# A perceiver block: order of small loads and scaled constants at two stage starts

## The chip, the cores and the metric

The kernel runs on one core of a Trainium2 chip. Its time is device time in microseconds (us) for one execution, as a median of several runs. A profiler trace of one such execution gives the start and duration of every instruction; all clock times below count from the start of that trace's span.

## The reference

One latent array x (512 rows of 512) attends to a context of 8192 rows, and then passes a state-space block, an MLP and a routed mixture of experts. Only the first part bears on this change:

```python
q = (scale * (layernorm(x) @ Wq + bq)).reshape(bs, q_len, NH, DM)     # 512 queries, 16 heads of 64
k = (ctx @ Wk + bk).reshape(bs, kv_len, NH, DM)                        # 8192 keys
v = (ctx @ Wv + bv).reshape(bs, kv_len, NH, DM)
a = softmax(einsum('nlhd,nshd->nhls', q, k), axis=-1)
x = x + einsum('nhls,nshd->nlhd', a, v).reshape(bs, q_len, NH * DM) @ Wo + bo
x = x + mamba_block(layernorm(x))                                      # scales by norm1_w first
x = x + mixture_of_experts(x)
```

Every float32 operand of a product is split into a float16 high part and a float16 rest, so a product is three float16 matmuls.

## The kernel before

The program is a row of stages. Each stage is one block in which all five engines run their own instruction lists, tied together by semaphores. A `Space` owns a stage's semaphores. When the stage ends, GpSimd clears them and all engines meet at a barrier (`Space.clear`, line 57), so nothing of the next stage starts before the last engine of this one is through, SyncE's waits for its transfers included. The order of work on each engine is the order in which its function is written. All DMAs that matter here are issued by SyncE and share one queue, which serves them in the order of issue.

**Latent queries** (`latent_queries`, names `lq_*` in the trace). SyncE loads x whole (line 130), then six halves of Wq, Wk and Wv into three buffers `wf` (line 135), with the query bias `bqc` behind the second half. From the fourth half on, a load waits until VectorE has split what lay in its buffer. Behind the sixth half come the key bias `bkc` (line 138) and the first two context chunks `cf[0]` and `cf[1]` (line 140). VectorE takes the row statistics of x (`row_factor`), normalises, and makes the float16 rests. ScalarE makes the float16 high parts. TensorE transposes x and computes eight pairs of heads (96 matmuls). For each pair j, ScalarE writes `qf` and its high part `qh[j]`, and VectorE the rest `ql[j]` (line 208). After the pairs, ScalarE and VectorE split the first context chunk (`keep.ch[0]`, line 180; `keep.cl[0]`, line 215), and VectorE scales the key bias (`keep.bks`, line 213). SyncE stores `qh` and `ql` to `q_dram` in two rounds, then waits at the end for both context chunks (`c_in`) and for the four stores (`q_out`, line 147).

**Context keys and values** (`context_keys_values`, names `kv_*`). TensorE works without a pause through 16 chunks. Its first product waits for `ch_ready`, `cl_ready` and `kf_ready`. At the stage's start VectorE raises semaphores by hand, one after another, to say that buffers are free; `ch_ready` and `cl_ready` are the thirteenth and the fourteenth (lines 437 and 438), `kf_ready` the first.

**Attention** (`attention`, names `at_*`). Each of 16 heads runs 32 steps (HP). In a step TensorE computes scores of 256 keys into one of three PSUM slots `st`, ScalarE exponentiates them into one of four buffers `pf` (line 734), ScalarE or VectorE makes the high part `ph` (line 728 or 772), VectorE the rest `pl` (line 776), and TensorE multiplies them with the values, four steps at a time. TensorE runs: scores of four steps, then values of the four steps before (`step`, called by `turns`). VectorE and ScalarE run `pair_turns`: the first CUT = 20 steps of head 0 straight, and everything else in a hardware loop over pairs of heads. SyncE loads head 0's queries, then four quarters of head 0's keys and values, then the queries of the other 15 heads, then the value bias `bvc` and the norm weight `nw` (both on semaphore `vec_in`), the output bias `bob`, and last a fill of `xs_dram` with zeros. Only then comes its loop that loads the next head's keys and values. VectorE waits for `vec_in`, scales the two vectors (`bvs`, `nws`, lines 763 and 764) and only then starts with step 0; ScalarE waits for `consts` before its step 0 (line 744). The scaled vectors are read for the first time at the end of the second head (`high` and `low`) and at the stage's end.

## Time and profile before

| | us |
|---|---|
| median of three runs | 2627.29 |
| lowest, highest | 2626.81, 2628.77 |
| the profiled execution's own time | 2626.91 |
| its span, first to last instruction | 2625.2 |
| TensorE busy | 2409.1 (92%) |
| VectorE busy | 1976.4 (75%) |
| ScalarE busy | 1595.8 (61%) |
| GpSimd busy | 683.3 (26%) |

The busy times are sums over stages with different limits. TensorE is nearly always at work inside the context stage and inside attention. What the change touches lies at their starts, where its busy share falls: the page's row of TensorE in 40 slices of 65.6 us reads 6 in the first slice and 1 in the fourteenth. Clock times in the text refer to this trace.

### The profile page before, as it was taken

The page shows a single profiled execution, that of the slowest core. Times are in us where ns is not written, and L with a number is a line of the kernel's source. Part 1 is how long each engine was busy: PE and PEld are TensorE (multiplying, and loading weights), DVE is VectorE, ACT ScalarE, POOL GpSimd, SP SyncE. Part 2 cuts the span into 40 slices and gives each one's busy share as a digit, 9 for nine tenths or more (in the row PEclk, how much of TensorE's full clock was granted, in tenths as well). Part 3 has the DMA queues.
Part 4 walks back from the last instruction along what each step waited for, and adds up shares of the span by engine and source line. Part 5 has one row for each costly group of instructions (what it writes and reads, how often), then busy time and mean ns, then how long its engine had stood idle before and what let it go on. Part 6 is the DMA issues. An engine that isn't in the chain of part 4 may idle for free. (4 is left out here: it accounts for less than half of the span.)

```text
span 2625.2 us, 39371 instructions
## 1 busy us (share of the span) xinstructions
PE 2409.1 (92%) x14143; PEld 1016.7 (39%) x14143; DVE 1976.4 (75%) x1974; ACT 1595.8 (61%) x1962; POOL 683.3 (26%) x475
## 2 busy tenths in 40 slices
...
GB/s 240 81 158 169 185 144 156 207 148 144 194 126 81 190 171 97 108 100 99 94 104 96 88 115 93 104 96 57 109 162 1 0 0 192 49 195 324 391 379 129
DMA packets 175780, 366.01 MB, mean 139 GB/s; under 512 B 17313, under 2 KB 88097, under 8 KB 172001
## 3 DMA queue, kind: packets, MB, share of 16 engines
...
HBM read 254.24 MB, written 106.68 MB: 137 GB/s over the span
## 5 line engine op out<-in xcount | busy, mean ns | idle before, releaser
L447 DVE TENSOR_REDUCE kv_mx<-kv_s 128x1024 f32 (+1 forms) x512 | 595.5, 1217 | 227.0 <-PE kv_s L477 227.0
L776 DVE TENSOR_TENSOR at_pl<-at_pf,at_ph 128x1024 f16<-128x1024 f32 x512 | 613.1, 1223 | 109.2 <-ACT at_ph L728 100.4
L734 ACT ACTIVATE at_pf<-at_st 128x1024 f32<-128x1024 f32 x512 | 497.0, 1025 | 213.2 <-PE at_st L893 119.3
L892 PE MATMUL at_st<-keep_big,at_k_cur 128*128 (+1 forms) x1024 | 392.2, 383 | 48.8 <-ACT at_pf L734 30.9
L893 PE MATMUL at_st<-keep_big,at_k_one 128*128 (+1 forms) x1024 | 390.7, 382 | 0.0
L728 ACT ACTIVATE at_ph<-at_pf 128x1024 f16<-128x1024 f32 x256 | 273.0, 1066 | 0.0
L1068 POOL MEMSET mi_xp<- 128x24 f32 x1 | 0.1, 123 | 977.8 <-POOLq L60 977.8
L857 PE MATMUL at_acc<-at_ph,at_vs 128*128 128x512 f16 x1024 | 242.4, 379 | 1.5 <-DVE at_pl L776 1.4
L367 POOL TENSOR_TENSOR kv_ksl<-kv_kf,kv_ksh 128x512 f16<-128x512 f32 x128 | 147.9, 1156 | 247.2 <-ACT kv_ksh L395 247.2
L993 PE MATMUL kv_kp<-first_ch,first_wkh 128*128 128x512 f16 x512 | 194.9, 381 | 8.8 <-DVEq L438 8.8
L993 PE MATMUL kv_kp<-first_ch,first_wkl 128*128 128x512 f16 x512 | 194.9, 381 | 0.0
L993 PE MATMUL kv_kp<-first_cl,first_wkh 128*128 128x512 f16 x512 | 194.6, 380 | 0.0
L993 PE MATMUL kv_vp<-first_wvl,first_ch 128*128 128x512 f16 x512 | 194.6, 380 | 0.0
L993 PE MATMUL kv_vp<-first_wvh,first_ch 128*128 128x512 f16 x512 | 194.5, 380 | 0.0
L993 PE MATMUL kv_vp<-first_wvh,first_cl 128*128 128x512 f16 x512 | 194.2, 379 | 0.0
L392 ACT ACTIVATE kv_kf<-kv_kp,first_bks 128x512 f32<-128x512 f32 x128 | 87.3, 682 | 172.3 <-PE kv_kp L993 172.3
L399 ACT ACTIVATE kv_vf<-kv_vp 128x512 f32<-128x512 f32 x128 | 76.0, 594 | 184.3 <-PE kv_vp L993 184.3
L1362 PE MATMUL ms_yp<-ms_hc,ms_ident 128*128 128x512 f32 x256 | 137.4, 684 | 51.2 <-POOL ms_hc L1248 42.6
L892 PEld LDWEIGHTS at_st<-keep_big,at_k_cur 128*128 128x128 f16 x1024 | 100.5, 98 | 211.2 <-issue 56.0
L371 POOL TENSOR_TENSOR kv_vs<-kv_vf,kv_vs 128x512 f16<-128x512 f32 x128 | 147.9, 1155 | 129.5 <-ACT kv_vs L401 129.5
L772 DVE CAST at_ph<-at_pf 128x1024 f16<-128x1024 f32 x256 | 175.5, 685 | 0.0
L1264 POOL TENSOR_TENSOR ms_b<-ms_u,keep_big 128x1024 f32<-128x1024 f32 x64 | 149.0, 2349 | 0.6
...
## 6 DMA issues: line engine op xcount, KB each, us to landing
...
at_k_cur<-kd SPq DMA_DIRECT2D x128, 256.0 KB, 3.9
at_vs<-vd SPq DMA_DIRECT2D x64, 512.0 KB, 3.9
kv_tf<-wpack SPq DMA_DIRECT2D x21, 1024.0 KB, 6.3
keep_big<-down SPq DMA_DIRECT2D x17, 1024.0 KB, 10.4
first_cf<-ctxT SPq DMA_DIRECT2D x16, 1024.0 KB, 13.2
kd<-kv_ksh SPq DMA_DIRECT2D x32, 512.0 KB, 9.8
```

The lines of the kernel that those rows point to most:

```text
L367: nc.gpsimd.tensor_tensor(ksl[par][:, n, :], kf[:, n % 4, :], ksh[par][:, n, :], ALU.subtract).then_inc(kl_ready, 1)
L371: nc.gpsimd.tensor_tensor(vs[par][:, hs, kt, DH:2 * DH], vf[:, n % 4, :].rearrange("p (h d) -> p h d", d=DH), vs[par][:, hs, kt, 0:DH], AL ...
L447: nc.vector.reduce_max(mx[:, bass.ds(g * (NH * TT) + 2 * (m - TT), 2)], s1[:, m % 3, :, :], AX.X).then_inc(s1_max, 1)
L728: nc.scalar.activation(ph[:, s % RING, :, :], pf[:, s % FULL, :, :], ACT.Copy).then_inc(ph_ready, 1)
L734: nc.scalar.activation(pf[:, s % FULL, :, :], st[:, s % HP % NST, :, :], ACT.Exp, scale=SCORE).then_inc(pf_ready, 1)
L772: nc.vector.tensor_copy(ph[:, s % RING, :, :], pf[:, s % FULL, :, :]).then_inc(ph_own, 1)
L776: nc.vector.tensor_tensor(pl[:, s % RING, :, :], pf[:, s % FULL, :, :], ph[:, s % RING, :, :], ALU.subtract).then_inc(pl_ready, 1)
L857: nc.tensor.matmul(acc[:, 0, :], vs[:, 2 * s + e, :], ph[:, s % RING, e, :], start=(s == 0 and e == 0), stop=False)
L892: nc.tensor.matmul(st[:, w % NST, e, :], k_cur[:, tile], qh[:, q], start=True, stop=False)
L893: last = nc.tensor.matmul(st[:, w % NST, e, :], k_one[:, tile], ql[:, q], start=False, stop=True)
L993: last = nc.tensor.matmul(out, a, b, start=(start and n == 0), stop=(stop and n == len(pairs) - 1))
L1264: nc.gpsimd.tensor_tensor(b[i % RB][:, :, :], u[:, :].unsqueeze(1).to_broadcast([P, HN, T]), bb[q], ALU.mult).then_inc(b_ready, 1)
```

## The change

In the latent stage, x is loaded in four pieces with a semaphore each, and the statistics of a piece wait for that piece alone. The first context chunk is loaded behind `bqc`, ahead of the third weight half, and is split between the weight halves 1 and 2. The key bias keeps its place behind the sixth half, but VectorE now waits for it and scales it ahead of the eight pairs. The second context chunk's load has its own semaphore. `ql` is no tensor of its own any more; it lies in the second chunk's buffers `keep.ch[1]` and `keep.cl[1]`. The wait for the stores of the queries leaves the stage: `q_out` becomes a semaphore of the whole program, and ScalarE waits for it in the context stage before it overwrites `keep.ch[1]`. Its `Space`, `whole`, is closed at the very end of the program. At the start of the context stage, `ch_ready` and `cl_ready` are raised first. In attention, `bvc` and `nw` are loaded ahead of the other heads' queries, and both the scaling on VectorE and ScalarE's wait for it come behind the first 20 steps.

```diff
@@ -107,18 +107,18 @@
-        qh, ql = keep.qh, m.sb("ql", [P, PAIRS, T], F16)
+        qh, ql = keep.qh, [(keep.ch if j < 4 else keep.cl)[1][:, j % 4, :] for j in range(PAIRS)]
...
-        x_in, b_in, made = m.sem("x_in"), m.sem("b_in"), m.sem("made")
+        x_in, b_in, made = [m.sem(f"x_in{t}") for t in range(TT)], m.sem("b_in"), m.sem("made")
@@ -127,24 +127,28 @@
-            sp.dma_start(xs[:, :, :], x.rearrange("(t p) d -> p t d", p=P)).then_inc(x_in, 16)
+            def load_context(n, sem):
+                sp.dma_start(keep.cf[n][:, :, :], ctxT.rearrange("(c p) s -> p c s", p=P)[:, :, n * CK:(n + 1) * CK]
+                             ).then_inc(sem, 16)
+
+            for t in range(TT):
+                sp.dma_start(xs[:, t, :], x[t * P:(t + 1) * P, :]).then_inc(x_in[t], 16)
             for n, (w, cols) in enumerate(halves):
+                if n == 2:
+                    load_context(0, c_in)
                 if n >= 3:
                     sp.wait_ge(wl_ready, n - 2)
                 src = (wq, wk, wv)[w].rearrange("(c p) n -> p c n", p=P)
                 sp.dma_start(wf[n % 3][:, :, :], src[:, :, cols]).then_inc(w_in[n % 3], 16)
                 if n == 1:
                     sp.dma_start(bqc[:, :], bq).then_inc(b_in, 16)
-            sp.dma_start(keep.bkc[:, :], bk).then_inc(c_in, 16)
-            for n in range(2):
-                sp.dma_start(keep.cf[n][:, :, :], ctxT.rearrange("(c p) s -> p c s", p=P)[:, :, n * CK:(n + 1) * CK]
-                             ).then_inc(c_in, 16)
-            for js in (slice(0, 4), slice(4, 8)):
+            sp.dma_start(keep.bkc[:, :], bk).then_inc(bk_in, 16)
+            load_context(1, next_in)
+            for js, low in ((slice(0, 4), keep.ch[1]), (slice(4, 8), keep.cl[1])):
                 sp.wait_ge(ql_ready, js.stop)
-                for s, q in enumerate((qh, ql)):
-                    sp.dma_start(q_dram[s].rearrange("(j p) t -> p j t", p=P)[:, js, :], q[:, js, :]).then_inc(q_out, 16)
-            sp.wait_ge(c_in, 48)
-            sp.wait_ge(q_out, 64)
+                for s, q in enumerate((qh[:, js, :], low[:, :, :])):
+                    sp.dma_start(q_dram[s].rearrange("(j p) t -> p j t", p=P)[:, js, :], q).then_inc(keep.q_out, 16)
+            sp.wait_ge(next_in, 16)
 
@@ -164,6 +168,8 @@
             split(1)
+            act.wait_ge(c_in, 16)
+            nc.scalar.activation(keep.ch[0][:, :, :], keep.cf[0][:, :, :], ACT.Copy, scale=SA).then_inc(ch_ready, 1)
             split(2)
@@ -176,8 +182,6 @@
                     split(3 + j // 2)
-            act.wait_ge(c_in, 48)
-            nc.scalar.activation(keep.ch[0][:, :, :], keep.cf[0][:, :, :], ACT.Copy, scale=SA).then_inc(ch_ready, 1)
@@ -189,8 +193,7 @@
-            dve.wait_ge(x_in, 16)
-            row_factor(nc, dve, own, xs, *rows.all, var_ready, sd_ready, 1, 1e-5, False)
+            row_factor(nc, dve, own, xs, *rows.all, var_ready, sd_ready, 1, 1e-5, False, x_in)
@@ -202,19 +205,18 @@
             split(1)
+            dve.wait_ge(ch_ready, 1)
+            nc.vector.scalar_tensor_tensor(keep.cl[0][:, :, :], keep.cf[0][:, :, :], SA, keep.ch[0][:, :, :],
+                                           ALU.mult, ALU.subtract)
             split(2)
+            dve.wait_ge(bk_in, 16)
+            nc.vector.tensor_scalar(keep.bks[:, :], keep.bkc[:, :], SA, None, ALU.mult)
             for j in range(PAIRS):
...
-                nc.vector.tensor_tensor(ql[:, j, :], qf[:, j % 4, :], qh[:, j, :],
+                nc.vector.tensor_tensor(ql[j], qf[:, j % 4, :], qh[:, j, :],
...
                     split(3 + j // 2)
-            dve.wait_ge(c_in, 48)
-            nc.vector.tensor_scalar(keep.bks[:, :], keep.bkc[:, :], SA, None, ALU.mult)
-            dve.wait_ge(ch_ready, 1)
-            nc.vector.scalar_tensor_tensor(keep.cl[0][:, :, :], keep.cf[0][:, :, :], SA, keep.ch[0][:, :, :],
-                                           ALU.mult, ALU.subtract)
@@ -403,6 +405,8 @@
                         nxt = 1 - par
+                        if i is None:
+                            act.wait_ge(keep.q_out, 64)
                         act.wait_ge(c_in[nxt], 16 * (uses + 1) + 16 * par)
@@ -424,6 +428,8 @@
+            dve.sem_inc(ch_ready, 1)
+            dve.sem_inc(cl_ready, 1)
             dve.sem_inc(kf_ready, 2)
@@ -434,8 +440,6 @@
                 dve.sem_inc(c_in[par], 16)
-            dve.sem_inc(ch_ready, 1)
-            dve.sem_inc(cl_ready, 1)
             for e in range(TW):
@@ -615,9 +619,9 @@
                 load_values(0, q)
-            load_queries(1, NH, q_rest_in)
             sp.dma_start(bvc[:, :], bv).then_inc(vec_in, 16)
             sp.dma_start(nw[:, :], n1w).then_inc(vec_in, 16)
+            load_queries(1, NH, q_rest_in)
             sp.dma_start(bob, bo.partition_broadcast(P)).then_inc(small_in, 16)
@@ -697,12 +701,13 @@
-        def pair_turns(eng, step, end, late):
+        def pair_turns(eng, step, end, late, once):
...
             for s in range(CUT):
                 step(0, s)
+            once()
             with eng.Fori(0, PAIRS - 1) as j:
@@ -741,8 +746,7 @@
-            act.wait_ge(consts, 2)
-            pair_turns(act, pair, lambda h: None, {HIGH_AT: high})
+            pair_turns(act, pair, lambda h: None, {HIGH_AT: high}, lambda: act.wait_ge(consts, 2))
@@ -759,10 +763,11 @@
             dve.sem_inc(o_out, 48)
-            dve.wait_ge(vec_in, 32)
-            nc.vector.tensor_scalar(bvs[:, :], bvc[:, :], SA, None, ALU.mult).then_inc(consts, 1)
-            nc.vector.tensor_scalar(nws[:, :], nw[:, :], SA, None, ALU.mult).then_inc(consts, 1)
-            dve.wait_ge(consts, 2)
+            def scaled():
+                dve.wait_ge(vec_in, 32)
+                nc.vector.tensor_scalar(bvs[:, :], bvc[:, :], SA, None, ALU.mult).then_inc(consts, 1)
+                nc.vector.tensor_scalar(nws[:, :], nw[:, :], SA, None, ALU.mult).then_inc(consts, 1)
+                dve.wait_ge(consts, 2)
@@ -803,7 +808,7 @@
-            pair_turns(dve, pair, end, {SUMS_AT: reciprocals, SCALE_AT: scale, LOW_AT: low})
+            pair_turns(dve, pair, end, {SUMS_AT: reciprocals, SCALE_AT: scale, LOW_AT: low}, scaled)
@@ -945,10 +950,12 @@
-def row_factor(nc, dve, own, src, st, mv, var, sd, rs, tmp, var_ready, sd_ready, n, eps, rms):
+def row_factor(nc, dve, own, src, st, mv, var, sd, rs, tmp, var_ready, sd_ready, n, eps, rms, rows_in=None):
 
 
     for t in range(TT):
+        if rows_in:
+            dve.wait_ge(rows_in[t], 16)
         own.inc(nc.vector.bn_stats(st[:, t, :], src[:, t, :]))
@@ -2150,6 +2157,8 @@
+    ending = ExitStack()
+    whole = Space(nc, ending, "whole")
@@ -2158,6 +2167,7 @@
+        keep.q_out = whole.sem("q_out")
@@ -2179,6 +2189,7 @@
         experts(nc, keep, xs_dram, ys_dram, wsplit, gate_up, down, out)
+    ending.close()
```

The rows below are the engines' instruction lists, before and after. Names in brackets are semaphores by the physical one that they share, so a name there can come from an earlier stage.

SyncE in the latent stage, from the query bias on, before:

```order
L137 DMA lq_bqc<-bq 128x8
L135 DMA lq_wf<-wk 128x4x512
L135 DMA lq_wf<-wk 128x4x512 [waits lq_wl_ready]
L135 DMA lq_wf<-wv 128x4x512 [waits lq_wl_ready] x2
L138 DMA first_bkc<-bk 128x8
L140 DMA first_cf<-ctxT 128x4x512 x2
L145 DMA q_dram<-first_qh 128x4x512 [waits lq_ql_ready]
L145 DMA q_dram<-lq_ql 128x4x512
L145 DMA q_dram<-first_qh 128x4x512 [waits lq_ql_ready]
L145 DMA q_dram<-lq_ql 128x4x512
L99 UNCONDITIONAL_BRANCH [waits lq_q_out,lq_c_in]
```

And after:

```order
L144 DMA lq_bqc<-bq 128x8
L131 DMA first_cf<-ctxT 128x4x512
L142 DMA lq_wf<-wk 128x4x512
L142 DMA lq_wf<-wk 128x4x512 [waits lq_wl_ready]
L142 DMA lq_wf<-wv 128x4x512 [waits lq_wl_ready] x2
L145 DMA first_bkc<-bk 128x8
L131 DMA first_cf<-ctxT 128x4x512
L150 DMA q_dram<-first_qh 128x4x512 [waits lq_ql_ready]
L150 DMA q_dram<-first_ch 128x4x512
L150 DMA q_dram<-first_qh 128x4x512 [waits lq_ql_ready]
L150 DMA q_dram<-first_cl 128x4x512
L99 UNCONDITIONAL_BRANCH [waits lq_next_in]
```

One context chunk now stands ahead of three weight halves, and at the stage's end the wait for the stores (`lq_q_out`) is gone.

VectorE in the latent stage, from the second weight half to the end of the stage, before:

```order
L189 SCALAR_TENSOR_TENSOR lq_wl<-lq_wf1,lq_wh 128x4x512 [waits lq_wh_ready]
L189 SCALAR_TENSOR_TENSOR first_wkl<-lq_wf2,first_wkh 128x4x512 [waits lq_wh_ready]
L208 TENSOR_TENSOR lq_ql<-lq_qf,first_qh 128x512 [waits lq_qh_ready] x2
L189 SCALAR_TENSOR_TENSOR first_wkl<-lq_wf0,first_wkh 128x4x512 [waits lq_wh_ready]
L208 TENSOR_TENSOR lq_ql<-lq_qf,first_qh 128x512 [waits lq_qh_ready] x2
L189 SCALAR_TENSOR_TENSOR first_wvl<-lq_wf1,first_wvh 128x4x512 [waits lq_wh_ready]
L208 TENSOR_TENSOR lq_ql<-lq_qf,first_qh 128x512 [waits lq_qh_ready] x2
L189 SCALAR_TENSOR_TENSOR first_wvl<-lq_wf2,first_wvh 128x4x512 [waits lq_wh_ready]
L208 TENSOR_TENSOR lq_ql<-lq_qf,first_qh 128x512 [waits lq_qh_ready] x2
L213 TENSOR_SCALAR first_bks<-first_bkc 128x8 [waits lq_c_in]
L215 SCALAR_TENSOR_TENSOR first_cl0<-first_cf0,first_ch0 128x2048 [waits lq_ch_ready]
```

And after (`first_ch1` and `first_cl1` are where `ql` lies now):

```order
L193 SCALAR_TENSOR_TENSOR lq_wl<-lq_wf1,lq_wh 128x4x512 [waits lq_wh_ready]
L209 SCALAR_TENSOR_TENSOR first_cl0<-first_cf0,first_ch0 128x2048 [waits lq_ch_ready]
L193 SCALAR_TENSOR_TENSOR first_wkl<-lq_wf2,first_wkh 128x4x512 [waits lq_wh_ready]
L213 TENSOR_SCALAR first_bks<-first_bkc 128x8 [waits lq_bk_in]
L216 TENSOR_TENSOR first_ch1<-lq_qf,first_qh 128x512 [waits lq_qh_ready] x2
L193 SCALAR_TENSOR_TENSOR first_wkl<-lq_wf0,first_wkh 128x4x512 [waits lq_wh_ready]
L216 TENSOR_TENSOR first_ch1<-lq_qf,first_qh 128x512 [waits lq_qh_ready] x2
L193 SCALAR_TENSOR_TENSOR first_wvl<-lq_wf1,first_wvh 128x4x512 [waits lq_wh_ready]
L216 TENSOR_TENSOR first_cl1<-lq_qf,first_qh 128x512 [waits lq_qh_ready] x2
L193 SCALAR_TENSOR_TENSOR first_wvl<-lq_wf2,first_wvh 128x4x512 [waits lq_wh_ready]
L216 TENSOR_TENSOR first_cl1<-lq_qf,first_qh 128x512 [waits lq_qh_ready] x2
```

The split of the chunk moves in among the weight halves, and the scaling of the key bias stands with its wait ahead of the first pair.

VectorE at the start of attention, from its barrier on, before (`kv_v_out1` is `vec_in`, `kv_v_out0` is `consts`):

```order
L753 UNCONDITIONAL_BRANCH [waits barrier_Pool_Activation_PE_DVE_SP_release]
L756 MEMSET keep_big 64x4096
L763 TENSOR_SCALAR at_bvs<-at_bvc 128x8 [waits kv_v_out1]
L764 TENSOR_SCALAR at_nws<-at_nw 128x4
L776 TENSOR_TENSOR at_pl<-at_pf,at_ph 128x1024 [waits lq_q_ready,kv_v_out0]
L772 CAST at_ph<-at_pf 128x1024 [waits lq_ql_ready,lq_b_ready]
L776 TENSOR_TENSOR at_pl<-at_pf,at_ph 128x1024 [waits lq_qf_ready]
```

And after, the same place:

```order
L757 UNCONDITIONAL_BRANCH [waits barrier_Pool_Activation_PE_DVE_SP_release]
L760 MEMSET keep_big 64x4096
L781 TENSOR_TENSOR at_pl<-at_pf,at_ph 128x1024 [waits lq_wl_ready]
L777 CAST at_ph<-at_pf 128x1024 [waits lq_q_ready,lq_wh_ready]
L781 TENSOR_TENSOR at_pl<-at_pf,at_ph 128x1024 [waits lq_own_dve]
```

VectorE after, around its twentieth step (the branch is the entry of the loop over pairs of heads):

```order
L777 CAST at_ph<-at_pf 128x1024 [waits lq_q_ready,lq_wh_ready]
L781 TENSOR_TENSOR at_pl<-at_pf,at_ph 128x1024 [waits lq_own_dve]
L768 TENSOR_SCALAR at_bvs<-at_bvc 128x8 [waits kv_v_out1]
L769 TENSOR_SCALAR at_nws<-at_nw 128x4
L711 UNCONDITIONAL_BRANCH [waits kv_v_out0]
L711 ISA
L781 TENSOR_TENSOR at_pl<-at_pf,at_ph 128x1024 [waits lq_wl_ready]
```

The two scalings move from the front to behind the twentieth step, and the wait for them now stands at the entry of the loop (the same on ScalarE).

## Rows read from the trace of the kernel before

**Rows 1.** Waits, 850 to 930 us: engine, waiting for what, total us, times, longest.

```profile
DVE at_bvs L763 <- DMA at_nw<-n1w: 38.3, 1, 38.3
ACT at_pf L734 <- DVE at_nws L764: 31.9, 1, 31.9
```

**Rows 2.** Timeline, attention start: start us, duration, engine, line, operation [idle before].

```profile
889.17 1.28 ACT L734 ACT_TABLE_LOAD   x1 [19.46 <-PE at_st L893]
891.90 14.83 SPq L597 DMA_DIRECT2D keep_big<-q_dram  x3
...
922.10 0.17 DVE L763 TENSOR_SCALAR at_bvs<-at_bvc 128x8 f32<-128x8 f32 x1 [38.34 <-DMA at_nw<-n1w]
922.38 1.94 ACT L734 ACTIVATE at_pf<-at_st 128x1024 f32<-128x1024 f32 x2 [31.92 <-DVE at_nws L764]
```

**Rows 3.** DMA issues at 911.43 and 913.38 us: KB each, us to landing.

```profile
at_nw<-n1w SPq DMA_DIRECT2D x1, 2.0 KB, 10.6
...
xs_dram<-at_none SPq DMA_DIRECT2D x1, 5888.0 KB, 23.7
```

**Rows 4.** DMA issue at 884.15 us, the first quarter of head 0's values.

```profile
at_vs<-vd SPq DMA_DIRECT2D x1, 512.0 KB, 6.2
```

**Rows 5.** Timeline: head 0's first product with values; exponentials of steps 32, 33.

```profile
929.87 0.38 PE L857 MATMUL at_acc<-at_ph,at_vs 128*128 128x512 f16 x1
...
977.80 1.94 ACT L734 ACTIVATE at_pf<-at_st 128x1024 f32<-128x1024 f32 x2 [1.48 <-DVE at_pl L776]
```

**Rows 6.** Timeline in a steady stretch of attention: VectorE, ScalarE, TensorE.

```profile
1021.21 1.22 DVE L776 TENSOR_TENSOR at_pl<-at_pf,at_ph 128x1024 f16<-128x1024 f32 x1
...
1020.56 1.94 ACT L734 ACTIVATE at_pf<-at_st 128x1024 f32<-128x1024 f32 x2 [1.48 <-DVE at_pl L776]
...
1022.01 0.38 PE L892 MATMUL at_st<-keep_big,at_k_cur 128*128 x1
```

**Rows 7.** GpSimd by lines, 879 to 896 us (busy us, mean ns); VectorE's timeline.

```profile
L680 POOL MEMSET at_k_one<- 64x2048 f16 x4 | 7.2, 1799 | 0.2
...
880.28 3.47 DVE L756 MEMSET keep_big<- 64x4096 uint32 x1 [11.42 <-PEq L60]
```

**Rows 8.** Timeline of VectorE in the first half of the latent stage.

```profile
6.45 2.47 DVE L952 BATCH_NORM_STATS2 lq_st<-lq_xs 128x6 f32<-128x512 f32 x4 [6.45 <-DMA lq_xs<-x]
...
12.72 0.16 DVE L198 TENSOR_SCALAR lq_bqs<-lq_bqc 128x8 f32<-128x8 f32 x1
...
18.85 2.29 DVE L189 SCALAR_TENSOR_TENSOR lq_wl<-lq_wf,lq_wh 128x2048 f16<-128x2048 f32 x1 [1.11 <-ACT lq_wh L158]
21.06 2.28 DVE L189 SCALAR_TENSOR_TENSOR first_wkl<-lq_wf,first_wkh 128x2048 f16<-128x2048 f32 x1
```

**Rows 9.** DMA issues at 2.41 us and at 23.4 us (the last weight half).

```profile
lq_bqc<-bq SPq DMA_DIRECT2D x1, 4.0 KB, 9.6
...
lq_wf<-wv SPq DMA_DIRECT2D x1, 1024.0 KB, 5.5
```

**Rows 10.** Timeline, latent stage's last pair to the next stage's first product.

```profile
38.31 0.38 PE L993 MATMUL lq_qp<-lq_xh,lq_wl 128*128 128x512 f16 x1
...
40.11 0.69 DVE L208 TENSOR_TENSOR lq_ql<-lq_qf,first_qh 128x512 f16<-128x512 f32 x1 [0.49 <-ACT first_qh L176]
...
41.23 0.51 SPq L145 DMA_DIRECT2D q_dram<-lq_ql  x1
...
46.14 0.20 POOL L75 MEMSET kv_ident<- 128x128 f32 x1 [44.60 <-POOLq L60]
...
47.49 0.58 PE L993 MATMUL kv_kp<-first_ch,first_wkh 128*128 128x512 f16 x1 [8.80 <-DVEq L438]
```

**Rows 11.** Waits of SyncE's queue between 0 and 60 us.

```profile
SPq L147 <- DMA q_dram<-lq_ql: 3.4, 1, 3.4
```

**Rows 12.** Windows: length, busy us of PE, PEld, DVE, ACT, POOL, granted clock, DMA.

```profile
38.70:43.00 4.30, 0.00 (x0) 0.00 (x0) 2.79 (x5) 3.11 (x3) 0.00 (x0) 1.00 0.30 99
...
47.40:50.00 2.60, 2.51 (x6) 0.87 (x7) 0.00 (x0) 0.00 (x0) 0.00 (x0) 0.50 0.76 306
```

4 lines of the change are left out of this document (2 added, 2 removed).

## The prediction

> **What bounds the kernel now.** Inside the context stage and inside attention TensorE runs without gaps, so only starts and ends of stages can give time back. I read the list of waits at the two places that the change touches, then the timeline there, then the transfers' times to landing.
>
> At the start of attention the list shows two waits in a chain [rows 1]: VectorE stands 38.3 us until `nw` lands, and ScalarE 31.9 us for VectorE's two small scalings. The reader is to see in the timeline [rows 2] that everything else was ready: ScalarE loads its exponential table at 889.17, right after the first scores, is done with it at 889.17 + 1.28 = 890.45, and starts the first exponential at 922.38. The cause is the queue. The queries of the 15 other heads are issued from 891.90 on and take 14.83 us to issue alone [rows 2], and `nw` lands 911.43 + 10.6 = 922.0 [rows 3]. TensorE can fill three slots and then waits as well.
>
> At the seam between the first two stages [rows 10] TensorE ends its last pair at 38.31 + 0.38 = 38.7 and starts the context stage at 47.49. What ends this: the last store of `ql` is issued by 41.74, SyncE waits 3.4 us for its landing [rows 11], 45.1; the barrier takes until 46.14; then VectorE raises fourteen semaphores by hand before TensorE may go, until 47.49.
>
> **Attention: the scalings leave the front.** The first exponential then waits only for its scores and the table: 890.45 in place of 922.38, **-31.9 us**. What is late next must not be a transfer. Head 0's own loads are issued before the moved ones and keep their times. The first product with values ran 929.87 - 922.38 = 7.5 us behind the first exponential [rows 5], so it comes at 897.9, and its quarter of values lands at 884.15 + 6.2 = 890.4 [rows 4]: 7.5 us of slack. Head 1's first keys are needed just before step 32, which ran at 977.80, 55.4 us behind the first exponential [rows 5], so at some 946. SyncE cannot issue them before it is through with the queries and the zero fill. The fill lands at 913.38 + 23.7 = 937.1 [rows 3] and is bound by bytes, not by issue, so it stays there; three quarter loads of 256 KB behind it need some 3 us, by half the 6.2 us of the 512 KB load [rows 4]. That is 940, 6 us in time. Moved with the fronts are only two tiny loads. Bounds: -30 (TensorE is still at half clock for a part of this) to -32.5.
>
> **Attention: the wait stands behind step 19 now.** On VectorE two operations of 0.17 us and their waits, 922.38 - 922.10 = 0.28 us [rows 2], come behind its twentieth step; queued behind them are its steps 20 on. ScalarE waits there for VectorE, which it otherwise never does this closely: in the steady rhythm ScalarE starts a new group of four at 1020.56 while VectorE ends the last step of the group before only at 1021.21 + 1.22 = 1022.43 [rows 6]. Step 20 opens a group. So its exponential starts at 1022.43 + 0.28 on that scale, 2.15 us late. TensorE's fourth score pair of that group needs it: it ran at 1022.01, and the exponential (half of 1.94, some 1.0) would have been done at 1021.6, 0.4 us earlier. So 1.75 us reach TensorE, which has no gap to win them back. The entry of the hardware loop, so far covered by ScalarE's idle 1.48 us per group, stands behind this wait too; I add 0.45 for it, between 0 and 1.5. Together **+2.2**, bounds 0.4 (if the rhythm at step 20 is looser than at step 60) and 3.3.
>
> **Latent stage: what ends it.** The pieces of x let VectorE take the statistics while x lands. The last piece lands when all of x does, at 6.45; three of four statistics of 2.47 us are then done, and the normalised rows come 1.85 us earlier. But the scaling of `bqc` at 12.72 waits for its load, 2.41 + 9.6 = 12.0 [rows 8, 9], so VectorE's chain behind it gains 0.7, at most 0.9 in TensorE's start. The stage's end does not see it, because of the new wait for `bk_in` on VectorE. `bkc` is issued behind the last weight half, in the same queue. That half was issued at 23.4, just behind VectorE's split of the third half (21.06 + 2.28), and took 5.5 us [rows 8, 9]. After the change VectorE has one chunk more to split there (2.21 us from start to start, 18.85 to 21.06) and starts some 1.9 earlier, so the half is issued at about 23.8 and lands at 29.3, `bkc` a little before or behind it; I take 29.0. Until then VectorE stands, with all eight `ql` and three weight splits queued behind: 8 x 0.60 + 3 x 2.21 = 11.4 us (from start to start: 0.69 less the 0.08 by which neighbours overlap at 21.06), so the last `ql` ends at 29.0 + 0.1 + 11.4 + 0.1 = 40.6. Before, it ended at 40.11 + 0.69 = 40.8 [rows 10]. TensorE and ScalarE pass this place with room (pair 7's `qf` needs only the `ql` of pair 3). So the end of the last `ql` moves by **-0.2**, bounds -0.9 (`bkc` lands early) and +1.0 (2 us late, half of it hidden). ScalarE's added 1.9 us of chunk split is hidden by its idle time between pairs.
>
> **The seam.** The stores are issued by 41.6 as before, but nothing waits for them: VectorE's 2.29 us and ScalarE's 1.89 us on the first chunk were under that wait already and are gone from the end as well. The barrier took 1.0 us from the last landing [rows 10, 11], so the context stage starts at 42.6 in place of 46.14: -3.4, besides the -0.2 above which is in it. The order of the hand-raised semaphores: fourteen took 47.49 - 46.14 = 1.35 us, of which three are left, 0.3: -1.05. Sum of latent stage and seam **-4.5**, bounds -3.3 and -5.7. The wait for `q_out` in the context stage comes on ScalarE behind its first key and value tile, some 8 us into the stage, when the stores (3.4 us) have landed: nothing.
>
> **Clock at the seam.** TensorE's pause shrinks from 8.8 to about 5 us. The granted clock was 1.00 in the first 4.3 us of the pause and 0.50, the lower of its levels of 1.2 and 2.4 GHz, when work resumed: six matmuls in 2.6 us instead of 1.3 [rows 12]. I count no change; if the shorter pause keeps the clock, 1.3 us more are won.
>
> **The end.** `whole` is cleared at the very end: one more clearing and one more barrier behind the last store. By the seam above at most 1.0 us; I take **+0.8**, bounds 0.3 and 1.0.
>
> **A rule weighed against the rows.** VectorE's casts and rests of the first steps, from about 892 on, now meet GpSimd's memsets, which run to 896. Rows 7 show VectorE's memset of 3.47 us from 880.28 across two or three of GpSimd's, while the four of line 680 take 1.80 us each on the mean, touched or not: no sign that one holds up the other, so the sum has 0 for it. The Trainium skill, SBUF — State Buffer, section "SBUF: two separate sides", says of the port pair that VectorE and GpSimd share that it is an exclusive lock and that whoever comes second blocks until the first is done. By that rule the first cast could wait for one memset.
>
> **Sum.** -31.9 + 2.2 - 4.5 + 0.8 = -33.4. From the profiled execution's own 2626.9 that is 2593.5; the median of the runs is 0.4 above it, so **2593.9 us**, 1.3% faster.
>
> **Rivals.**
> - Transfers become the bound of head 0 or of head 1's start. For it: the queue is full from 881 to 937, and the shortest slack is 6 us. Against it: what is needed first is issued first and keeps its place. If the fill and the keys behind it came 14 us late, 8 would show: 2602.
> - A lock between VectorE and GpSimd at 892 to 896, the rule above: one memset of 1.80 us [rows 7] on VectorE, 2595.7.
> - The clock stays up over the shorter seam: 2592.6.
> - The first exponential waits for something that the list of waits hides, since a wait for several semaphores is put down to the last of them, and the change at attention doesn't do what it says. Then only the rest is left: 2626.9 - 4.5 + 2.2 + 0.8 + 0.4 = 2625.8, no change. Against it: the table load, behind the scores' semaphore, started at 889.17.
> - Slower: the pushed wait at step 20 throws three engines out of their rhythm and they settle in a slower one. Steady groups have TensorE without a gap, and ScalarE 1.48 us idle. From a loss of 0.27 us per group over the 123 groups behind step 20 the gain is gone; at 0.35 the time is 2593.9 + 43 = 2637. Against it: three slots and four buffers take up such a push, and TensorE's order is fixed.
>
> **Chances.** Forecast 0.75, clock stays 0.08, lock 0.05, transfers 0.07, does not act 0.02, slower rhythm 0.03. A measurement here can tell about 0.2%, 5 us, from no change. Faster 0.95, same 0.02, slower 0.03. Range: the sum of the good bounds, -32.5 + 0.4 - 5.7 + 0.3 = -37.5, with 1.3 of clock less, would be 2588.5, of the bad ones -30 + 3.3 - 3.3 + 1.0 = -29.0, 2598.3. Not all fall on one side, and a part of the transfers' case is let in above: 2589.5 to 2600.
>
> **What would show it.** The wait list at the start of attention has no row of 31.9 us; ScalarE's first exponential starts 1.3 us behind the first scores. Before step 20's exponential ScalarE idles some 3.5 to 4 us for VectorE. VectorE idles about 5 us in the latent stage ahead of `bks`, and the first product of the context stage starts near 43. Wrong would be: keys or values named before TensorE in heads 0 and 1, or idle time of TensorE in every group of four.

## The result, and the profile after

The changed kernel takes **2593.12 us** in the median of four runs (2591.79 to 2599.14), the kernel before 2628.03 on the same chip (2626.81 to 2629.07). The ratio is 0.9872, with a 95% interval of 0.9855 to 0.9889: 1.3% faster. On a second chip it was 2596.09 against 2628.09, ratio 0.9879 (0.9863 to 0.9896). The profiled execution took 2591.8 us, its span 2590.1.

The list of waits at the start of attention in the changed kernel, first 876 to 930 us (engine, line, waiting for what: total us, times, longest):

```profile
PE at_st L897 <- DMA keep_big<-m_dram: 18.8, 1, 18.8
POOL at_ones L681 <- POOLq L60: 17.7, 1, 17.7
DVE at_pl L781 <- ACT at_ph L733: 16.0, 5, 10.2
ACT at_pf L739 <- PE at_st L898: 14.5, 5, 9.5
...
ACT at_pf L739 <- DVE at_nws L769: 3.8, 1, 3.8
```

The two waits of [rows 1], 38.3 and 31.9 us, are gone. What ScalarE waits for now are the scores, and once, for 3.8 us, the scaled vectors. The timeline of SyncE, ScalarE and GpSimd there:

```profile
889.67 0.43 SPq L623 DMA_DIRECT2D at_nw<-n1w  x1
890.14 13.59 SPq L601 DMA_DIRECT2D keep_big<-q_dram  x3
...
908.91 0.71 SPq L627 DMA_DIRECT2D xs_dram<-at_none  x1
910.02 17.28 SPq L607 DMA_DIRECT2D at_k_cur<-kd  x2
```

```profile
887.55 1.02 ACT L739 ACTIVATE at_pf<-at_st 128x1024 f32<-128x1024 f32 x1 [9.48 <-PE at_st L898]
889.25 1.02 ACT L739 ACTIVATE at_pf<-at_st 128x1024 f32<-128x1024 f32 x1 [0.68 <-PE at_st L898]
```

The stage starts at 876.62 (GpSimd's first row, below), 2.74 us earlier than before, and the first exponential at 887.55 in place of 922.38. The keys of head 1 stand behind the zero fill in the queue, issued from 910.02 on. The list above ends before they are needed; the same list taken for 876 to 1100 us has no wait of TensorE for keys or values either, only 18.8 us for `m_dram` at the start, 2.1 for exponentials and 0.2 for rests. Around step 20, ScalarE and VectorE:

```profile
919.90 1.08 ACT L733 ACTIVATE at_ph<-at_pf 128x1024 f16<-128x1024 f32 x1
924.76 1.94 ACT L739 ACTIVATE at_pf<-at_st 128x1024 f32<-128x1024 f32 x2 [3.78 <-DVE at_nws L769]
```

```profile
923.10 1.23 DVE L781 TENSOR_TENSOR at_pl<-at_pf,at_ph 128x1024 f16<-128x1024 f32 x1
924.24 0.16 DVE L768 TENSOR_SCALAR at_bvs<-at_bvc 128x8 f32<-128x8 f32 x1
924.32 0.16 DVE L769 TENSOR_SCALAR at_nws<-at_nw 128x4 f32<-128x4 f32 x1
927.68 1.23 DVE L781 TENSOR_TENSOR at_pl<-at_pf,at_ph 128x1024 f16<-128x1024 f32 x1 [3.20 <-ACT at_ph L733]
```

The vectors landed long before; VectorE scales them as soon as it is through with step 19, and ScalarE, which had run ahead of it, has stood 3.78 us by then.

Latent stage and seam, VectorE and then TensorE and SyncE:

```profile
9.59 1.92 DVE L198 TENSOR_SCALAR lq_xn<-lq_xs,lq_mv,lq_rs 128x512 f32<-128x512 f32 x4
12.71 0.17 DVE L201 TENSOR_SCALAR lq_bqs<-lq_bqc 128x8 f32<-128x8 f32 x1 [1.20 <-DMA lq_bqc<-bq]
...
29.72 0.17 DVE L213 TENSOR_SCALAR first_bks<-first_bkc 128x8 f32<-128x8 f32 x1 [5.26 <-DMA first_bkc<-bk]
...
41.53 0.69 DVE L216 TENSOR_TENSOR first_cl<-lq_qf,first_qh 128x512 f16<-128x512 f32 x1 [0.48 <-ACT first_qh L182]
```

```profile
17.52 0.61 PE L1000 MATMUL lq_qp<-lq_xh,lq_wh 128*128 128x512 f16 x1 [2.22 <-DVE lq_xl L205]
17.92 0.63 PE L1000 MATMUL lq_qp<-lq_xl,lq_wh 128*128 128x512 f16 x1
...
44.57 0.38 PE L1000 MATMUL kv_kp<-first_ch,first_wkh 128*128 128x512 f16 x1 [4.46 <-DVEq L433]
```

```profile
42.65 0.51 SPq L150 DMA_DIRECT2D q_dram<-first_cl  x1
```

The first product of the context stage comes at 44.57, before at 47.49 [rows 10]. `bqs` is made at 12.71, where it was made before at 12.72 [rows 8]: in spite of the pieces of x nothing is won there. The first eight matmuls of the pairs stand 0.40 to 0.43 us apart, twice the 0.22 of before. A window at the start of the context stage (length, busy us, granted clock, DMA share, GB/s) has ten matmuls in 3.40 us at a granted clock of 0.50, the lower level:

```profile
44.90:48.30 3.40, 3.40 (x10) 1.22 (x8) 0.00 (x0) 0.00 (x0) 0.00 (x0) 0.50 1.02 318
```

### The profile page after: what moved, and what is told of

The parts are those of the page before. It is cut to its first block and busy times, and to the rows that moved or that the text cites. A ratio compares the mean times of both kernels' runs of the same rounds, so it can differ in the third digit from the quotient of the medians.

```text
span 2590.1 us, 39386 instructions
## 1 busy us (share of the span) xinstructions
PE 2405.5 (93%) x14143; PEld 1015.6 (39%) x14143; DVE 1976.4 (76%) x1974; ACT 1596.4 (62%) x1962; POOL 683.5 (26%) x475
## 5 line engine op out<-in xcount | busy, mean ns | idle before, releaser
L897 PE MATMUL at_st<-keep_big,at_k_cur 128*128 (+1 forms) x1024 | 391.3, 382 | 20.8 <-DMA keep_big<-m_dram 18.8
```

The lines of the kernel that those rows point to most:

```text
L897: nc.tensor.matmul(st[:, w % NST, e, :], k_cur[:, tile], qh[:, q], start=True, stop=False)
```

## The accounts

Each row below is a difference between two traces, read off the timelines; the first column is the trace shown ahead of the prediction against the one above, the second a pair taken together on the second chip (the runs `before_again` and `after_again` below). "Step n" is the start of ScalarE's exponential of step n.

| | predicted | first pair | second pair |
|---|---|---|---|
| latent stage and seam, to the first product | -4.5 | -2.92 | -5.07 |
| from there to attention's start | 0 | +0.18 | +0.54 |
| attention's start to step 0 | -31.9 | -32.09 | -33.67 |
| steps 0 to 16 | 0 | +0.93 | +0.81 |
| steps 16 to 24 | +2.2 | +1.88 | +1.88 |
| step 24 to the mixer's start | 0 | +0.61 | +0.42 |
| mixer, its output, experts, to the end | +0.8 | -3.69 | -1.41 |
| span | -33.4 | -35.1 | -36.5 |

The last row but one holds the extra barrier: from the issue of the last store to the end it was 2625.2 - 2622.0 = 3.2 before and is 2590.1 - 2586.5 = 3.6 now, **+0.4**. The rest of it, about -4.1 in the first pair, is in stages that the change doesn't touch. The row above it (+0.61, +0.42) lies within the scatter of that stretch, which took 909.8 to 910.8 us in all 14 traces. The second row has a cause, the clock: from the first product on, the context stage works at half clock for 2.7 us in the trace of before (47.49 to 50.15) and 3.4 in the changed kernel (to 48.31), and for 3.3 and 4.8 us in the second pair. Half of the differences, 0.4 and 0.7, is what that should cost, by estimate.

## Experiments

### The two parts, each alone

`e1_attention_only` has the changed attention (the loads of `bvc` and `nw` ahead, the scaling behind 20 steps) and the old latent stage, seam and end; `e2_latent_only` has the rest of the change and the old attention. The diff is that of `e2` against the changed kernel, without VectorE's part, whose scalings go back to the front as well:

```diff
-            sp.dma_start(bvc[:, :], bv).then_inc(vec_in, 16)
-            sp.dma_start(nw[:, :], n1w).then_inc(vec_in, 16)
             load_queries(1, NH, q_rest_in)
+            sp.dma_start(bvc[:, :], bv).then_inc(vec_in, 16)
+            sp.dma_start(nw[:, :], n1w).then_inc(vec_in, 16)
...
-            pair_turns(act, pair, lambda h: None, {HIGH_AT: high}, lambda: act.wait_ge(consts, 2))
+            act.wait_ge(consts, 2)
+            pair_turns(act, pair, lambda h: None, {HIGH_AT: high})
```

> Only the attention part of the change: the two small loads ahead of the other heads' queries, the scalings and ScalarE's wait behind step 19. The latent stage, the hand-raised semaphores and the end are those of before. Theory (the gain is the wait of the first exponential, less a push at step 20): the first exponential some 11 us behind the start of the attention stage in place of 43, one idle of ScalarE of 3.8 us ahead of step 20, and a gain at step 24 of 29 to 30 us; time 2596 to 2599 from 2628. Rival (the latent part carries more than its 3 us, say by what it does to later stages): 2601 or more here.

> Only the latent part of the change with the semaphores' order and the semaphore of the whole program; attention is that of before. Theory: the context stage's first product 2.9 us earlier, or up to 4.5 where TensorE's clock rises in the latent stage as early as before the change; 0.4 back at the end; time 2623.5 to 2625.5 from 2628, so hardly more than the runs scatter. Rival (the whole change scatters because this part disturbs the clock): runs spread over more than 3 us here.

Attention alone: ratio 0.9901 (0.988 to 0.9922). Latent stage, seam and end alone: 0.9979 (0.9968 to 0.9991). The product is 0.9880, the whole change 0.9872 and 0.9879: the parts add up within these intervals. Two numbers did not come as expected. The median of `e1` is 2601.49 us (four runs, 2597.15 to 2605.08), outside the 2596 to 2599 of its theory and inside its rival's 2601 or more. And the ten runs of `e2` spread over 8.9 us, which its rival had as the sign of a disturbed clock; the kernel before spreads over 10.1 us in 13 runs on the same chip, so the spread says nothing of the change. The times alone leave `e1` a gain between 20 and 32 us; that attention carries its 30 is shown by the traces. In them the first exponential of `e1` comes 9.54 us behind the stage's start (before: 43.02), and step 24 comes 53.85 us behind it, where before it took 84.19 and 84.86, so 30.3 to 31.0 us less; the first product of `e2` comes at 44.95, where the two kernels with the old stage, `e1` and `before_again`, have 49.73 and 49.81.

### Is it the order of the loads, or the place of the scaling?

`e3_old_loads` is the changed kernel with `bvc` and `nw` loaded behind the other heads' queries again (the first two lines of the diff above). `e4_front_scaling` keeps them ahead, and scales and waits ahead of step 0 again (the last lines of it).

> The changed kernel with the two small loads put back behind the 15 heads' queries; the scalings stay behind step 19. Theory (putting the scalings late is what acts): nw lands some 43 us behind the start of the attention stage, as before the change, and VectorE asks for it at 47.6, so ScalarE's idle time ahead of step 20 stays 3.8 us and the time is that of the changed kernel within its scatter, 2591 to 2599. Rival (the order of loads acts too): ScalarE idles longer than 5 us ahead of step 20, and the time rises by that.

> The changed kernel with the scalings and the wait for them back at the front of attention; the two small loads stay ahead of the other heads' queries. Theory (the queue serves in order of issue): nw is issued behind head 0's quarters and lands with the last of them, some 27 to 29 us behind the start of the stage, so the first exponential starts there in place of 11 (changed) and 43 (before). There is no push at step 20. Time 2591.8 + 17 - 2.8, some 2606 to 2608. Rival (small loads overtake large ones): the first exponential at 11 to 15, 2590.

`e3` starts step 0 10.88 us behind the stage's start, as the changed kernel does (10.93), and reaches step 24 at 931.00 against 931.53: the order of the loads gives nothing once the scaling is late. `e4` starts it 28.93 us behind. Its ScalarE and VectorE:

```profile
906.01 1.94 ACT L738 ACTIVATE at_pf<-at_st 128x1024 f32<-128x1024 f32 x2 [17.46 <-DVE at_nws L768]
```

```profile
905.73 0.17 DVE L767 TENSOR_SCALAR at_bvs<-at_bvc 128x8 f32<-128x8 f32 x1 [24.26 <-DMA at_nw<-n1w]
```

In `e4` `nw` is issued at 890.26 and its scaling starts at 905.73, 15.5 us later, for 2 KB: it lands behind head 0's keys and values, which are in the queue ahead of it. So of the 32 us, loading first would have won 14 and scaling late wins all. Each was run once, in 2599.65 us (`e3`, expected 2591 to 2599) and 2611.01 (`e4`, expected 2606 to 2608); both times came out above what was expected, and the reading rests on the traces.

### The push at step 20

`e5_wait_at_use`: ScalarE waits for the constants where it reads them.

```diff
             def high(j):
+                act.wait_ge(consts, 2)
...
-            pair_turns(act, pair, lambda h: None, {HIGH_AT: high}, lambda: act.wait_ge(consts, 2))
+            pair_turns(act, pair, lambda h: None, {HIGH_AT: high}, lambda: None)
```

> The changed kernel with one move: ScalarE no longer waits for the scaled constants behind step 19 but inside `high`, where it reads them first; VectorE scales them behind step 19 as before. Theory: the longer four steps before step 20 (9.44 us for steps 16 to 20 in the changed kernel, 7.20 before) are ScalarE's wait for VectorE, so here steps 16 to 20 take 7.2 us, steps 20 to 24 take 7.1, and step 24's exponential comes 1.9 us nearer to the stage's start. Rival: VectorE's queue is what is late, and the steps stay at 9.4 or the same 2 us show in the next four. In the total 1.9 us, 0.07%, which may not be told from the scatter of later stages.

```profile
923.97 1.06 ACT L733 ACTIVATE at_ph<-at_pf 128x1024 f16<-128x1024 f32 x1
924.92 1.94 ACT L739 ACTIVATE at_pf<-at_st 128x1024 f32<-128x1024 f32 x2
```

ScalarE goes from step 19 into step 20 without a pause. Steps 16 to 20 take 7.20 us and 20 to 24 7.13, as before the change (7.20 and 7.13; changed kernel 9.44 and 6.77). The push is ScalarE's wait and nothing else, 1.88 us; VectorE's two operations in the same place (923.86 and 923.94) cost nothing. In the total it can't be seen: ratio 0.9882 (0.9865 to 0.9898).

### The latent stage

`e7_x_whole` loads x in one DMA. `e8_bias_early` loads both biases right behind x:

```diff
+            sp.dma_start(bqc[:, :], bq).then_inc(b_in, 16)
+            sp.dma_start(keep.bkc[:, :], bk).then_inc(bk_in, 16)
             for n, (w, cols) in enumerate(halves):
...
-                if n == 1:
-                    sp.dma_start(bqc[:, :], bq).then_inc(b_in, 16)
-            sp.dma_start(keep.bkc[:, :], bk).then_inc(bk_in, 16)
```

> The changed kernel with x loaded by one DMA, as before. Theory: the pieces bring the normalised rows 1.3 us nearer, but VectorE waits 1.0 to 1.2 us for the query bias behind them, so loading whole costs 0 to 0.3 us: the split of the first weights starts at 12.7 to 13.1 and the first pair at 17.5 to 18.0. Rival: the pieces do bring the first pair forward by the 0.7 to 0.9 us of the prediction, and it starts at 18.3 or later here.

> The changed kernel with one move: both biases, `bqc` and `bkc`, are loaded right behind x, ahead of all weights. Theory: the pieces of x gave nothing because VectorE then waited 1.20 us for `bqc`, and the key bias cost VectorE 5.26 us ahead of the pairs because it stands behind six weight halves. Then neither wait shows here; the split of the first weights and TensorE's first pair start 0.7 to 1.1 us earlier than 17.5, at 16.4 to 16.8, or the weights become the bound, if two small loads ahead of them delay them by as much. The scaled key bias stands near 24 instead of 29.7, and the stage's end moves by the pairs' start alone, since the last rests of the queries wait for ScalarE. Rival: the 5.26 us of standing make the stage's end late; then the end moves by 2 us or more.

> The kernel before, traced once more. Asked: whether the trace shown above is typical at the eight pairs, whose matmuls stood 0.22 us apart from the first one on there and 0.43 us apart for the first eight in the changed kernel. Theory: the half clock from about 17.5 to 21 us depends on the execution and not on how x is loaded (the kernel with the attention part alone, which loads x whole, has it too), so it can show here; then the pairs last 22.5 to 23 us instead of 20.9 and the first product starts near 49 to 49.5. Rival: loading x whole keeps the clock up, and the pairs last 20.9 us again. Later stages give a spread: from the mixer's start to the output stage 296 to 299 us, experts to the end 302 to 310.

| trace | first pair starts | pairs end | took | last `ql` ends | behind the pairs |
|---|---|---|---|---|---|
| before | 17.80 | 38.69 | 20.9 | 40.80 | 2.11 |
| `before_again` | 17.94 | 41.01 | 23.1 | 43.12 | 2.11 |
| `e1` (old latent stage) | 18.00 | 40.93 | 22.9 | 43.04 | 2.11 |
| after | 17.52 | 40.12 | 22.6 | 42.22 | 2.10 |
| `after_again` | 17.70 | 40.29 | 22.6 | 42.39 | 2.10 |
| `e7_x_whole` | 17.96 | 38.86 | 20.9 | 42.56 | 3.70 |
| `e8_bias_early` | 16.79 | 39.37 | 22.6 | 41.47 | 2.10 |

Three things follow. **The clock.** The same code ran the pairs in 20.9 and in 23.1 us (before, `before_again`). The difference is the spacing of the matmuls at the start of the pairs, of the first ten here and of the first eight to thirteen in other traces:

```profile
17.94 0.61 PE L993 MATMUL lq_qp<-lq_xh,lq_wh 128*128 128x512 f16 x1 [1.42 <-DVE lq_xl L202]
18.34 0.63 PE L993 MATMUL lq_qp<-lq_xl,lq_wh 128*128 128x512 f16 x1
```

```profile
17.96 0.39 PE L999 MATMUL lq_qp<-lq_xh,lq_wh 128*128 128x512 f16 x1 [1.42 <-DVE lq_xl L204]
18.19 0.38 PE L999 MATMUL lq_qp<-lq_xl,lq_wh 128*128 128x512 f16 x1
```

The first two rows are `before_again`, the last two `e7`. Where the record of the granted clock reaches back so far, the wide spacing is the lower level: in `after_again` 0.50 from 18.8 to 22.1 us, 1.00 before and behind. Of 14 traces 12 have the wide spacing near the start of the pairs, in four of them only from the third to sixth matmul on, and their pairs last 22.5 to 23.7 us; the trace shown ahead of the prediction is one of the two that haven't. It made the latent stage of before look 2.2 us shorter than it is most of the time. Loading x whole isn't the reason, for `before_again` and `e1` load it whole too.

**The pieces of x** brought the first pair 0.24 to 0.28 us forward (17.96 and 17.94 against 17.70; 17.80 against 17.52), not 0.7 to 0.9: `bqc` landed when VectorE had already waited 1.20 us for it. Even the 0.28 can't be told from scatter, for the eight traces with x in pieces and the biases in their places start the first pair at 16.57 to 18.02, the four with x whole at 17.80 to 18.00. The pieces themselves push `bqc`: SyncE issues three more DMAs ahead of it, so that it is issued at 3.71 instead of 2.41. With the biases ahead (`e8`) that wait is gone and another takes its place, for the weights that now come behind two small loads. VectorE, ScalarE and SyncE of `e8`, and SyncE of the changed kernel:

```profile
10.67 0.17 DVE L200 TENSOR_SCALAR lq_bqs<-lq_bqc 128x8 f32<-128x8 f32 x1
12.04 2.29 DVE L192 SCALAR_TENSOR_TENSOR lq_wl<-lq_wf,lq_wh 128x2048 f16<-128x2048 f32 x1 [1.21 <-ACT lq_wh L161]
```

```profile
10.10 1.91 ACT L161 ACTIVATE lq_wh<-lq_wf 128x2048 f16<-128x2048 f32 x1 [2.38 <-DMA lq_wf<-wq]
```

```profile
3.63 0.98 SPq L144 DMA_DIRECT2D lq_wf<-wq  x2
```

```profile
2.68 0.98 SPq L142 DMA_DIRECT2D lq_wf<-wq  x2
```

From the start of ScalarE's first split, which follows the landing of the first weights, to the first pair it takes 6.69 us in `e8` (and in `e9` below), and 7.71 to 7.75 in the eight traces with the changed order: the wait for `bqc` was worth 1.0. But the first weights are issued 0.95 us later, at 3.63 instead of 2.68, so nearly all of it is given back on the way. `e8` starts its pairs at 16.79, as expected, yet that lies inside the 16.57 to 18.02 of the changed order; in one execution a gain of this size can't be seen.

**The wait for the key bias** was expected to show or not, by theory, in the stage's end. Both happened. In `e7`, at full clock, VectorE works without a pause from `bks` to the last `ql`:

```profile
30.98 0.17 DVE L212 TENSOR_SCALAR first_bks<-first_bkc 128x8 f32<-128x8 f32 x1 [5.27 <-DMA first_bkc<-bk]
31.06 1.29 DVE L215 TENSOR_TENSOR first_ch<-lq_qf,first_qh 128x512 f16<-128x512 f32 x2
...
41.27 1.29 DVE L215 TENSOR_TENSOR first_cl<-lq_qf,first_qh 128x512 f16<-128x512 f32 x2
```

That is 42.56 - 30.98 = 11.58 us, and the last `ql` ends 3.70 us behind the pairs instead of 2.11: the wait costs 1.6. A part of that is `e7`'s own, since `bks` comes 1.26 us later there than in the changed kernel (30.98 against 29.72). At full clock the changed kernel's pairs would end near 17.52 + 20.9 = 38.4, and the wait would cost some 0.8 (an estimate: 29.72 + 11.58 = 41.3 against 38.4 + 2.1). In the changed kernel and `after_again`, with the slow start of the pairs, the queue has caught up at the last pair and the wait costs nothing; `e8`, which has no such wait, ends its last `ql` just as far behind the pairs (2.10).

### The seam

`e10_q_wait` puts SyncE's wait for the four stores back; `e11_sems_late` puts the two hand-raised semaphores back behind twelve others.

```diff
             sp.wait_ge(next_in, 16)
+            sp.wait_ge(keep.q_out, 64)
...
-            dve.sem_inc(ch_ready, 1)
-            dve.sem_inc(cl_ready, 1)
             dve.sem_inc(kf_ready, 2)
...
                 dve.sem_inc(c_in[par], 16)
+            dve.sem_inc(ch_ready, 1)
+            dve.sem_inc(cl_ready, 1)
```

> The changed kernel with the wait for the four stores of the queries put back at the end of the latent stage. Theory: the stage's end stands behind the last store's landing; from the last rest of the queries to the next stage's start 5.3 us instead of 1.98, so 3.4 us later there (start near 47.6 for rests that end near 42.2) and 3.4 us in the total. Rival: the second context chunk, whose wait stays in both, lands last, and the start of the next stage moves by less than 1 us.

> The changed kernel with the two hand-raised semaphores for the first context chunk put back behind twelve others. Theory: the first product starts 0.37 us behind the stage's start in the changed kernel and 1.35 us before it, and this order alone is the difference; so 1.3 to 1.4 us here. Rival: the earlier product comes from the shorter wait list of TensorE or from the barrier, and it stays near 0.4.

`e10`, SyncE's last store, GpSimd's first row of the next stage, TensorE's first product; then GpSimd and TensorE in `e11`:

```profile
43.72 0.51 SPq L150 DMA_DIRECT2D q_dram<-first_cl  x1
...
48.81 0.20 POOL L75 MEMSET kv_ident<- 128x128 f32 x1 [47.27 <-POOLq L60]
...
49.19 0.59 PE L1001 MATMUL kv_kp<-first_ch,first_wkh 128*128 128x512 f16 x1 [8.01 <-DVEq L434]
```

```profile
45.46 0.20 POOL L75 MEMSET kv_ident<- 128x128 f32 x1 [43.91 <-POOLq L60]
...
46.81 0.59 PE L1000 MATMUL kv_kp<-first_ch,first_wkh 128*128 128x512 f16 x1 [5.43 <-DVEq L442]
```

From the last `ql` to the next stage it is 5.52 us with the wait (`e10`), 1.98 without (after), 5.34 before. From the stage's start to the first product it is 1.35 us with the old order (`e11`, and before) and 0.37 with the new one. Both edits do what they were costed at. One trace each; their totals (2603.57 and 2592.53 us, a single run) can't tell 1 us. In `e10` the first context chunk is loaded and split early and the seam is as long as before, so the early split wins nothing as long as the wait for the stores stands. The other half, no wait and the split still at the stage's end, was not run.

### A version of both

> The changed kernel once more, beside the next one on one chip. Theory: 1.3% faster than before, ratio 0.985 to 0.989. In the trace the marks of the first 930 us lie within 1 us of the first one's, the later stages scatter by some us.

> The changed kernel with ScalarE's wait for the constants at their first use and both biases loaded right behind x. Theory: 1.9 us from the push at step 20 and 0 to 0.3 us from the biases, ratio to before 0.0007 lower than that of the changed kernel, which is inside both intervals; in the trace steps 16 to 20 take 7.2 us and VectorE stands for neither bias. Rival: the two edits give more than their sum because VectorE's work in the latent stage gets 5.3 us of room, which brings the end of that stage forward; then the next stage starts at 43.0 or earlier relative to pairs that start at 17.5.

`e9_best` (the edits of `e5` and `e8` together) has a median of 2595.72 us and a ratio of 0.9874 (0.9858 to 0.9891), the changed kernel beside it 2596.09 and 0.9879 (0.9863 to 0.9896): not told apart. The 1.9 us at step 20 are won (steps 16 to 20 in 7.21), and in this execution the first weights landed later still, ScalarE's split of them starting at 11.98, so that the first pair started at 18.67, again 6.69 us behind. They took 8.3 us from issue to landing, against 6.4 in `e8` and 6.1 to 7.6 with the changed order; what delayed them stays open.

## Who holds up whom: VectorE and GpSimd

The prediction had 0 for a lock between VectorE and GpSimd, and a rival at 1.8 us. The traces show it. GpSimd and VectorE in the changed kernel:

```profile
876.62 0.12 POOL L681 MEMSET at_ones<- 128x32 f16 x1 [17.69 <-POOLq L60]
...
889.80 1.80 POOL L685 MEMSET at_k_one<- 1x2048 f16 x1
891.65 0.96 POOL L686 MEMSET at_none<- 128x1024 f16 x1
...
892.91 0.53 POOL L77 TENSOR_SCALAR_AFFINE_SELECT at_ident<-at_ident 128x128 f32<-128x128 f32 x1 [0.16 <-POOL at_ident L75]
```

```profile
891.25 1.23 DVE L781 TENSOR_TENSOR at_pl<-at_pf,at_ph 128x1024 f16<-128x1024 f32 x1 [10.25 <-ACT at_ph L733]
892.40 0.91 DVE L777 CAST at_ph<-at_pf 128x1024 f16<-128x1024 f32 x1
```

and in `after_again`:

```profile
892.36 1.42 POOL L686 MEMSET at_none<- 128x1024 f16 x1
...
894.09 1.35 POOL L77 TENSOR_SCALAR_AFFINE_SELECT at_ident<-at_ident 128x128 f32<-128x128 f32 x1 [0.16 <-POOL at_ident L75]
```

```profile
892.21 0.69 DVE L777 CAST at_ph<-at_pf 128x1024 f16<-128x1024 f32 x1
892.93 2.36 DVE L781 TENSOR_TENSOR at_pl<-at_pf,at_ph 128x1024 f16<-128x1024 f32 x2
```

In the first the memset was there first (891.65 to 892.61), and the cast ends 0.69 us behind it, its own length: 893.30. In the second the cast was there first (892.21 to 892.90), and the memset, 0.96 us long when alone, takes 1.42. The identity's select, which reads SBUF, takes 0.29 us when alone (before). In the first trace it came while the cast ran and takes 0.53, in the second it came while the second rest ran and takes 1.35; both times it ends 0.14 us behind the VectorE operation. But a rest of 1.23 us beside a memset of 1.80 stretches neither (891.25 and 889.80 above). The Trainium skill, SBUF — State Buffer, section "SBUF: two separate sides", says just that when read to its end: the lock is taken by a VectorE operation in a two-port mode against any GpSimd operation, and by one with two SBUF inputs only against a GpSimd operation that reads SBUF. The traces agree, with the numbers above; that the cast ran in such a mode no trace shows.

What it costs can be read from ten traces with the late scaling, since the memset of `at_none` starts 15.03 to 15.04 us behind the stage's start in all of them. Where the first cast was issued before it (`e1`, `e7`, `e10`, `e11`, `after_again`), step 16 starts 37.64 to 37.71 us behind the stage's start. Where it was issued with it or later (after, `e3`, `e5`, `e8`, `e9`), the cast ends at 16.68, however early it was issued, and step 16 starts at 38.70, **1.05 us later**. So 0.14 us between two casts (14.90 in `e10`, 15.04 in `e9`) decide on a microsecond. The first casts of `e9` and `e1`:

```profile
893.10 1.64 DVE L777 CAST at_ph<-at_pf 128x1024 f16<-128x1024 f32 x1
```

```profile
895.97 1.22 DVE L773 CAST at_ph<-at_pf 128x1024 f16<-128x1024 f32 x1
```

The stretch of the cast beyond its own 0.69 is the lock's own share: 0.95 us in `e9` (1.64), 0.92 in `e5` (1.61), 0.84 in `e8`, 0.55 in `e3`, and 0.22 in the changed kernel's first trace, whose cast came at 15.78 anyway. The memset ahead of `at_none` can hold it up too: in `e1` the cast was issued at 14.30 beside the last one of `at_k_one` (13.17 to 14.97) and took 1.22, 0.53 over its own, in `e7` 0.92 and in `e11` 0.78. In the traces where `at_none` came second, the late select holds up the second cast, 0.78 instead of 0.69. So the lock takes 0.1 to 1 us, never the 1.8 of the rival. No kernel with the memset elsewhere was run.

With this the 16 steps can be added up. In all 14 traces step 16 starts 22.02 to 22.12 us behind the end of the first cast, before and after. From step 0 to the start of that cast it takes 4.13 us where three slots of scores stand full (before, `before_again`, `e2`, `e4`) and 4.85 in the two traces of the changed kernel. That is +0.72 for the scores and +0.22 for the lock in the first, +0.72 and +0.1 in the second, which are the +0.93 and +0.81 of the table.

## Why the prediction was right, step by step

- **What bounds attention's start, right.** First exponential -31.9 predicted, -32.09 and -33.67 measured. It follows the first scores, which themselves start 9.00 us behind the stage's start instead of 7.85 in the first trace (8.09 against 8.17 in the second pair). The table load, taken as part of the path with its 1.28 us, is no longer on it: in the changed kernel it stands right at the stage's start, at 876.78. So -32.09 is luck in part, two misses of 1.28 and 1.15 us against each other; where the scores came as early as before, the gain was 33.67, outside the bounds of -30 to -32.5.
- **Not in the sum: the ramp.** Steps 0 to 16 take 0.8 to 0.9 us more. Before, three slots of scores stood full and the first exponentials ran back to back [rows 2]; now the second waits 0.68 for its scores, at half clock (granted clock 0.50 from 862 to 890), which gives 0.72, and VectorE meets GpSimd. The bound of -30 on the first term had left room for it, the value taken had not. The lock was priced at 0 and took 0.22 in the profiled execution, 0.1 to 0.95 in others. The step that failed is the reading of [rows 7] as no sign of it: they show a VectorE memset, not the cast that would stand there.
- **Push at step 20, right:** +2.2 predicted, +1.88 measured, 1.75 of it worked out from the steady rhythm. The 0.45 for the loop's entry is not needed; `e5` shows 7.20 and 7.13 with the entry in its place.
- **Latent stage, size off.** `ql` end -0.2 predicted, +1.42 measured against the trace shown, and -0.73 for `after_again` against `before_again`. With it the sum of latent stage and seam, -4.5 with bounds -3.3 and -5.7, came at -2.92, outside, and at -5.07. The working of VectorE's queue was right where it was tried: 11.5 to 11.6 us from `bks` to the end predicted, 11.58 in `e7`. `bkc` landed at 29.7, not 29.0. The step that failed is that this queue ends the stage. In the changed kernel it would have been through at 41.3, and TensorE's last pair, 22.6 us behind the first instead of 20.9, ended it at 42.2. What was missing is that the pairs' clock is not the same in each execution, and that it decides which of the two ends the stage.
- **x in pieces, wrong:** 0.7 to 0.9 predicted for the first pair, 0.24 to 0.28 measured; `bqc` was taken to land at 12.0 as before and landed at 12.7. That step overlooked what the pieces do to SyncE's own list, where they put `bqc` 1.3 us back.
- **Seam, right:** from the last `ql` to the next stage 2.0 us predicted (40.6 to 42.6), 1.98 measured, 5.34 before; semaphores -1.05 predicted, -0.98 measured. The prediction's own difference, 42.6 against 46.14, is -3.5, and its sum goes on with -3.4. **The clock there:** counted as no change. The first matmul ran at full clock, and then half clock lasted for more of the work than before, 3.4 us instead of 2.7. The rival, a clock that stays up, did not come.
- **End:** +0.8 predicted, +0.4 measured.
- **Transfers, slower rhythm:** neither came. From step 24 to the mixer's start it took 910.14 and 910.42 us in the traces of before, 910.75 and 910.84 in those of the changed kernel, and TensorE waits for no keys or values there.
- **The last 750 us**, not in the sum: mixer's start to its output 296.4 to 299.3 us, experts to the end 299.8 to 309.7, over 14 traces of kernels that are the same there but for the last barrier. Four us fell to the changed kernel in the first pair. That the median came within 1 us of the forecast is therefore luck in part; on the second chip it was 2.2 above. A part goes with TensorE's clock: in the experts its busy time is 272.5 to 279.7 us, and three of the four longest executions (307.1 to 309.7) have a mean granted clock of 0.95 to 0.96, the shortest (299.8) has 0.98. The rest stays open, for at 0.98 the length still varies from 299.8 to 308.4.
